# An fp32 metaformer block: the first stage written out as a pipeline over image pairs, and raw x turned to token order through the centring matrix

## What is computed

```python
def reference(x, ...):                       # x: (32, 64, 56, 56) fp32
    x = x + conv_ref(_ln_c(x), weight, gamma, beta, bn_mean, bn_var)
    t = _to_tokens(x)                        # (32, 3136, 64)
    t = t + ffn_ref(_ln_t(t), sigma, phi, M_u, M_phi_plus, M_phi_minus, log_weights, gumbel)
    return _from_tokens(t, x)

def conv_ref(x, ...):                        # its residual is the normalized x
    out = sign(x)
    out = conv3x3(out, scale * sign(weight)) # padding 1
    return out * inv[c] + (beta - mean * inv)[c] + x

def ffn_ref(x, ...):                         # a spectral unit: FFT convolution of length 4096 over
    ...                                      # the tokens with 16 filters, a 64x64 matrix for each
```

## Time and profile before

| | us |
|---|---|
| median of three runs | 1637.34 (1632.1 to 1641.38) |
| the profiled execution | 1645.81, its span 1643.9 |
| prepare | 0 to 61.8 |
| first stage | 61.8 to 760.1 |
| mixing stage: preparing M, then the units | 760.1 to 796.5, then to about 1340 |
| busy over the span | PE 80%, DVE 67%, ACT 50%, POOL 40% |

### The profile page before, as it was taken

How to read it: one execution, slowest core, us unless ns; L and a number is a source line. 1 busy time by engine, 2 the same in 40 slices (tenths; PEclk the granted TensorE clock), 3 DMA queues, 4 the chain that set the end, 5 groups by cost and what they waited for, 6 DMA issues and landing times. The chain is left out here.

```text
span 1643.9 us, 36604 instructions
## 1 busy us (share of the span) xinstructions
PE 1320.2 (80%) x13633; PEld 902.3 (55%) x13633; DVE 1098.6 (67%) x1492; ACT 815.8 (50%) x1517; POOL 659.5 (40%) x665
## 2 busy tenths in 40 slices
PE   1467888888888888867897999999999991867756
PEld 1244444444444444432686898998998980433323
DVE  5268888888888888886665777775776760433323
ACT  0344666666666666644554565564565650222222
POOL 1046777777777777760012232322323222000000
PEclk9988999999999999985798999999999996878888
DMA  9911334434444334335189998997989876987883
GB/s 144 70 70 65 129 128 129 129 131 130 129 129 132 129 132 129 108 100 154 56 231 270 279 288 261 272 261 218 276 252 269 264 217 215 362 345 273 345 338 159
DMA packets 187818, 317.15 MB, mean 193 GB/s; under 512 B 23029, under 2 KB 162647, under 8 KB 171159
## 3 DMA queue, kind: packets, MB, share of 16 engines
q1 hardware_dynamic: 173190, 257.40, 52.9%
q0 software_dynamic: 14592, 59.26, 10.0%
HBM read 162.86 MB, written 153.76 MB: 193 GB/s over the span
## 5 line engine op out<-in xcount | busy, mean ns | idle before, releaser
L939 POOL DMA_DIRECT2D w_scratch<-wf x256 | 151.3, 595 | 467.2 <-ACT y_sb L1117 406.7
L998 PE MATMUL ring<-v_mov,m_sta 105*128 105x128 f16 x4096 | 234.0, 219 | 0.0
L998 PEld LDWEIGHTS ring<-v_mov,m_sta 105*128 105x128 f16 x4096 | 231.5, 98 | 0.4
L554 PE MATMUL p_conv<-signs_padded,conv_w 128*128 128x448 bf16 x1008 | 198.2, 354 | 11.7 <-ACT conv_y L620 11.7
L658 POOL TENSOR_TENSOR conv_y<-conv_y,x_in 128x448 f32<-128x448 f32 x112 | 180.5, 1626 | 40.1 <-ACT conv_y L620 32.6
L1134 DVE COPY hf<-ring 128x512 f32<-128x512 f32 x256 | 168.7, 689 | 26.8 <-PE ring L998 25.8
L1117 ACT ACTIVATE hf<-ring 128x512 f32<-128x512 f32 x256 | 153.0, 598 | 58.6 <-PE ring L998 56.7
L526 PE MATMUL p_rt<-ident,conv_y 128*98 128x128 f32 x512 | 92.0, 319 | 96.9 <-DVE x_t L739 53.9
L1267 PE MATMUL p_out<-w_in,last_masked 128*98 128x512 f32 x256 | 143.4, 645 | 25.4 <-DMA w_in<-w_scratch 25.4
L1323 ACT ACTIVATE out_sb<-p_turn 128x392 f32<-128x392 f32 x128 | 62.7, 498 | 196.6 <-PE p_turn L1279 188.2
L554 PEld LDWEIGHTS p_conv<-signs_padded,conv_w 128*128 128x128 bf16 x1008 | 96.6, 97 | 115.6 <-issue 18.9
(11 more groups left out here) (140 smaller groups left out, 2228.4 us busy)
## 6 DMA issues: line engine op xcount, KB each, us to landing
z_in<-z_scratch SPq DMA_DIRECT2D x32, 1076.5 KB, 8.4
z_scratch<-z_sb SPq DMA_DIRECT2D x16, 2048.0 KB, 8.9
y_scratch<-y_sb SPq DMA_DIRECT2D x32, 1024.0 KB, 9.2
yt<-y_scratch SPq DMA_DIRECT2D x64, 512.0 KB, 6.5
w_scratch<-wf POOLq DMA_DIRECT2D x256, 128.0 KB, 5.4
w_in<-w_scratch SPq DMA_DIRECT2D x8, 4096.0 KB, 15.0
x_in<-in_x SPq DMA_DIRECT2D x16, 1568.0 KB, 11.0
x_scratch<-x_t SPq DMA_DIRECT2D x16, 1568.0 KB
```

The lines of the kernel that those rows point to most:

```text
L554: mm = nc.tensor.matmul(p_conv[:, c % 2, 0:CW], keep["conv_w"][:, t, :], pad[:, rows, t % 3:t % 3 + WID], start=(t == 0), stop=(t == 8))
L939: nc.gpsimd.dma_start(w_units[u, h, s, c], wf[64 * c:64 * c + 64, 2 * h + s].rearrange("p (g n) -> p g n", n=256)).then_inc(w_stored, 16)
L998: mm = nc.tensor.matmul(bank[:, 2 * NF * i:2 * NF * i + 2 * NF], m_sta[:, 2 * e + 1 - n:2 * e + 3 - n, :].rearrange("k b d -> k (b d)"), v ...
```

## The change

**The loop.** The first stage is written out without loops, in 20 turns (`TURNS`, -2 to 17). Turn `it` convolves pair `it`, turns x of pair `it+1` to token order, centres pair `it+2` for its signs, finishes the second normalization of pair `it-1` and makes step 1 of pair `it-2`.

**Raw x.** `x_cen` and its seven copies a pair are gone. `turn_x` makes, in place of each transpose of centred x, a product of raw x (stationary) with the centring matrix (moving), which centres and turns at once. x of three pairs is held in `x_all`; its rows are overwritten in place by the residual.

**Work on other engines.** ScalarE's seven scalings and GpSimd's seven additions of the residual become one bias on the whole pair on ScalarE (`add_bias`) and seven operations on VectorE (`residual`), which read the convolution from PSUM. Both roots of a turn are made together on 128 columns: a square root on ScalarE, a reciprocal and three small steps on VectorE. The scaling of `xc_t` moves from VectorE (2 x 2048 columns) to GpSimd (4 x 1024), both squarings of u are on ScalarE, step 1 goes through `p_xt`.

**The ends.** In `prepare` the three filter stores are one with rows three times as long, a third x is loaded, and the loads of M go to the end of turn 14. The maxima of M stand on VectorE behind the last pair.

The diff, cut to what is spoken of:

```diff
-        filt_z = sb("filt_z", [NROW, NA, NK])
+        filt_z = sb("filt_z", [NROW, NA, 3, NK])
...
-            for q in range(2):
-                sp.dma_start(keep["x_in"][q][:], x_pairs[q]).then_inc(keep["x_loaded"][q], 16)
-
-            sp.wait_ge(filt_saved, 4)
-            for copy_of in range(3):
-                at = NIMG * CH + NK * copy_of
-                sp.dma_start(d["z"][:, :, at:at + NK], filt_z[:]).then_inc(filt_stored, 16)
-            for row, n, src in ((0, KF, d["M_plus"]), (KF, KF, d["M_minus"]), (2 * KF, KU, d["M_u"])):
-                for i in range(NBR):
-                    rows, m = slice(i * NK + row, i * NK + row + n), src[i].rearrange("k d e -> k (d e)")
-                    if i < NBR - 1:
-                        sp.dma_start(keep["m_raw"][0][rows, :], m).then_inc(keep["m_loaded"], 16)
-                    else:
-                        for h in range(2):
-                            sp.dma_start(keep["m_raw"][1][KI * h + row:KI * h + row + n, :],
-                                         m[:, h * M_COLS // 2:(h + 1) * M_COLS // 2]).then_inc(keep["m_loaded"], 16)
-            sp.wait_ge(filt_stored, 48)
+            for q in range(3):
+                sp.dma_start(keep["x_all"][:, TOK * q:TOK * q + TOK], x_pairs[q]).then_inc(keep["x_loaded"][q], 16)
+
+            sp.wait_ge(filt_saved, 12)
+            sp.dma_start(d["z"][:, :, NIMG * CH:ZCOLS], filt_z[:].rearrange("p a t k -> p a (t k)")
+                         ).then_inc(filt_stored, 16)
+            sp.wait_ge(filt_stored, 16)
...
-                nc.vector.tensor_copy(filt_z[:, 8 * c:8 * c + 8, :].rearrange("p a k -> p (a k)"),
-                                      p_f[:, c, 0:8 * NK]).then_inc(filt_saved, 1)
+                for t in range(3):
+                    nc.vector.tensor_copy(filt_z[:, 8 * c:8 * c + 8, t, :],
+                                          p_f[:, c, 0:8 * NK].rearrange("p (a k) -> p a k", k=NK)
+                                          ).then_inc(filt_saved, 1)
...
+            for it in TURNS:
+                if there(it - 2):
+                    sp.wait_ge(z_saved, NTOK * (it - 2) + NTOK)
+                    sp.dma_start(d["z"][:, :, 128 * (it - 2):128 * (it - 2) + 128],
+                                 z_sb[:].rearrange("p c (a n) -> p (c a) n", n=128)).then_inc(z_stored, 16)
+                if not there(it):
+                    continue
+                if there(it + 3):
+                    sp.wait_ge(rt_ready, NTOK * it + NTOK)
+                    sp.dma_start(x_of(it + 3), x_pairs[it + 3]).then_inc(x_loaded[it % 3], 16)
+                sp.wait_ge(x1_done, NTOK * it + NTOK)
+                sp.dma_start(d["x1"][it], x1_t[:].rearrange("p c n -> p (c n)")).then_inc(x1_stored, 16)
+                if it == NPAIR - 2:
...
+            def turn_x(q, c):
...
+                if c < 2 and there(q - 4):
+                    pe.wait_ge(z_saved, NTOK * (q - 4) + NTOK - 1 + c)
+                elif NTOK * q + c >= 2:
+                    pe.wait_ge(xt_copied, NTOK * q + c - 1)
+                    pe.wait_ge(xt_squared, NTOK * q + c - 1)
+                for j in range(ACH):
+                    a = ACH * c + j
+                    mm = nc.tensor.matmul(p_xt[0:NB, c % 2, 128 * j:128 * j + 128], x_of(q)[:, a:TOK:NA],
+                                          keep["center"][:], start=True, stop=True)
+                mm.then_inc(xt_ready, 1)
...
+            def step1(q, c):
+
+                if c >= 2 or not there(q + 3):
+                    if NTOK * q + c >= 2:
+                        pe.wait_ge(z_saved, NTOK * q + c - 1)
+                else:
+                    pe.wait_ge(xt_copied, NTOK * (q + 3) + NTOK - 1 + c)
+                    pe.wait_ge(xt_squared, NTOK * (q + 3) + NTOK - 1 + c)
+                if c % 2 == 0:
+                    if q == NPAIR - 1 and c >= 4:
+                        pe.wait_ge(u_last, c // 2 - 1)
+                    else:
+                        pe.wait_ge(u_done, 4 * q + c // 2 + 1)
+                nc.tensor.matmul(p_xt[:, c % 2, :], keep["step1"][:, c // 2, :], u_t[q % 2][:, c, :],
+                                 start=True, stop=True).then_inc(z_ready, 1)
+
...
+            for it in TURNS:
+                for c in range(NCONV):
+                    if there(it):
+                        convolve(it, c)
+                    if c < 4 and there(it + 1):
+                        turn_x(it + 1, 2 * c)
+                        turn_x(it + 1, 2 * c + 1)
+                    if c >= 4 and there(it - 2):
+                        for k in range(3 * (c - 4), min(3 * (c - 4) + 3, NTOK)):
+                            step1(it - 2, k)
...
+                    if c < NCONV and there(it + 2):
+                        center(it + 2, c)
+                    if there(it):
+                        turn_r(it, c)
...
+            def square2(q, h):
+
+                if h == 0:
+                    act.wait_ge(u_centered, q + 1)
+                else:
+                    act.wait_ge(u_centered_late, 2 * q + 2)
+                if there(q - 1):
+                    act.wait_ge(ssq2_done, 2 * (q - 1) + h + 1)
+                v = slice(HALF * h, HALF * h + HALF)
+                nc.scalar.activation(sq2[:, v, :], u_t[q % 2][:, v, :], ACT.Square).then_inc(sq2_done, 1)
+
+            def add_bias(q):
+
+                act.wait_ge(cen_ready, NCONV * q + NCONV)
+                act.wait_ge(xt_ready, NTOK * q + NTOK)
+                nc.scalar.activation(x_of(q), x_of(q), ACT.Identity, bias=keep["bn"][:, 1:2]).then_inc(biased, 1)
+
             def save_z(q, c):
...
+            def square_root(it):
+
+                s = roots_of(it)
+                act.wait_ge(var_done, it + 2)
+                nc.scalar.activation(deviation[:, s], var[:, s], ACT.Sqrt).then_inc(deviation_done, 1)
+
+            for it in TURNS:
+                if there(it + 1):
+                    for c in range(NTOK):
+                        copy_x(it + 1, c)
+                if there(it - 1):
+                    for h in range(2):
+                        square2(it - 1, h)
+                if there(it + 1):
+                    add_bias(it + 1)
+                if there(it - 2):
+                    for c in range(NTOK):
+                        save_z(it - 2, c)
...
+                    if there(it + 2):
+                        signs(it + 2, c)
+                    if c == 1 and (there(it + 1) or there(it - 1)):
+                        square_root(it)
...
+                if there(it - 2):
+                    q = it - 2
+                    pool.wait_ge(root_done, it + 1)
+                    for c in range(4 if q < NPAIR - 1 else 2):
+                        scaled_by_root(nc.gpsimd, u_t[q % 2], c, 64).then_inc(u_done, 1)
+                if there(it - 1):
+                    q = it - 1
+                    pool.wait_ge(mean2_done, q + 1)
+                    if there(q - 2):
+                        pool.wait_ge(z_ready, NTOK * (q - 2) + NTOK)
+                    for c in (2, 3):
+                        v = slice(2 * c, 2 * c + 2)
+                        nc.gpsimd.tensor_tensor(u_t[q % 2][:, v, :].rearrange(groups, n=CH),
+                                                x1_t[:, v, :].rearrange(groups, n=CH),
+                                                mean2[:, 16 * c:16 * c + 16].unsqueeze(2).to_broadcast([NB, 16, CH]),
+                                                ALU.subtract).then_inc(u_centered_late, 1)
+                if there(it):
+                    pool.wait_ge(root_done, it + 1)
+                    for c in range(4):
+                        scaled_by_root(nc.gpsimd, xc_t[it % 2], c, 0).then_inc(normed, 1)
             pool.wait_ge(peaks_done, len(M_PIECES))
             nc.gpsimd.partition_all_reduce(keep["peak"][:], keep["peaks"][:], 128, bass.bass_isa.ReduceOp.max)
...
+            def residual(q, c):
+
+                g = NCONV * q + c
+                if c == 0:
+                    dve.wait_ge(biased, q + 1)
+                dve.wait_ge(conv_ready, g + 1)
+                v = x_of(q)[:, CW * c:CW * c + CW]
+                nc.vector.scalar_tensor_tensor(v, p_conv[:, g % 2, 0:CW], keep["bn"][:, 0:1], v,
+                                               ALU.mult, ALU.add).then_inc(r_done, 1)
+
...
+            for it in TURNS:
+                before, now, after = there(it - 1), there(it), there(it + 1)
+                if before:
+                    mean_sum(it - 1, 0)
+                if now:
+                    residual(it, 0)
+                if before:
+                    mean_sum(it - 1, 1)
+                    mean_scale(it - 1)
+                if now:
+                    residual(it, 1)
+                if before:
+                    center_u(it - 1)
+                if now:
+                    residual(it, 2)
+                if after:
+                    sums1(it + 1, 0)
+                if now:
+                    residual(it, 3)
+                if after:
```

(22 more changed lines are left out.)

428 lines of the change are left out of this document (153 added, 275 removed).

## The result

The changed kernel takes 1679.4 us (median of 4 runs, 1674.3 to 1683.5) against 1637.5 for the kernel before: a ratio of 1.026, 95% interval 1.021 to 1.030. It is slower by 42 us where I forecast 14 us faster, outside my range of 1598 to 1644. Its profiled execution took 1674.3 us (span 1672.6), and I read that one.

The account below looks back on a forecast made before the run. Bound: first stage a loop of handoffs, none of its engines full. Prologue -21.8, pairs +2.6, -9.2, +10.4, -2.3, -5.8, drain +12.0: -14.1 us, from 1645.8 to 1632, carried to the median 1623; own range 1611 to 1636, overall 1598 to 1644.

Parts of the forecast that it names:

- The step that failed: TensorE's turn of x: 64 product instructions at 0.12 us each, 7.6 us, priced by the forward transform.
- The second term: TensorE's half clock after its stall before the third step-1 product: 1.3 us a turn, of the 1.5 it costs now.
- Rival 1: Handoff costs less: TensorE's clock stays up, turn 40.5 us, gain 17 us, time 1606; chance 0.25.
- rival 2: GpSimd and VectorE lock each other out around the late centring: turn 43.6 us, time 1647; chance 0.17.
- rival 3: Prologue gains only half, 10 of 21.8 us, and the drain runs at half clock (+4): 1639; chance 0.08.
- The stall: TensorE stands 4.6 us before the third step-1 product, waiting for ScalarE's save behind two squarings and the bias.
- The bias: ScalarE's one bias operation on 3136 columns a pair: 2.75 us, by the line through copy and squaring.
- No lock from the residual additions: VectorE's seven residuals a turn, one operand in PSUM, add no wait with GpSimd: 0.65 us each.
- The late centring: GpSimd's half of centring u, ending 15.0 us into the turn, 2.3 us before the second squaring wants it.
- The start of the stage: First stage starts at 40 us after one filter store and no M loads, 21.8 us earlier; VectorE's end 34.5.
- The drain: End of the first stage after the last x1 store: 43.2 us, 12.0 more, with the maxima of M last.
- M's preparation: Stretch after the first stage's drain, 36.4 us in the kernel before: taken as untouched, no change.

Follow-up runs that it names:

- the filled stall: Changed kernel plus 18 additional bf16 matmuls a turn on TensorE, between the second and third product of step 1: 1648.9 us.
- the last version: Changed kernel with centred copy kept and transposed, ScalarE's queue reordered, and two residual additions moved up in VectorE's queue: 1508.9 us, ratio 0.924 to the kernel before.
- the product alone: Kernel before, with its transposes of centred x replaced by the product of raw x with the centring matrix and ScalarE's seven copies dropped: 1667.4 us, ratio 1.020.
- the centred copy: Changed kernel, but ScalarE copies each centred chunk out of PSUM and 32 transposes of that copy replace the raw product: 1592.3 us, ratio 0.976.
- both repairs: Changed kernel with the centred copy kept and transposed, and ScalarE's bias and saves put ahead of the squarings: 1523.5 us, ratio 0.932.

## Why the prediction was wrong

**The step that failed** is one term of the sum: "the nearest row of the same shape is the forward transform, 15 in 1.94 us, 0.12 each: 64 of them, 7.6". The shape was nearly the same (the same moving side, 128 stationary columns there and 98 here), the walk through memory was not: the forward transform reads its stationary columns side by side, the product of raw x 32 words apart. In the profile of before the only strided stationaries were those of transposes, and they were no slower than others, so I had a reason not to ask; but the rows did not show a strided one in a true product, and a price that they don't show should have been bounded on both sides. The 64 instructions measured 10.64 us, 0.166 each: 3.04 a turn more, 37 of the 50 us in the twelve pairs. With the columns side by side they take 7.0, so the stride alone makes the difference. In pair 0, where the products run twice, it is some 6.3 of the 7.9 (11.25 for the first 64, from 48.00 to 59.25, where I had 8).

**The second term was mis-sized**: the half clock at 1.3 us, taken from the some 3 us at half clock that followed the old stall of 2.73. Behind the one of 4.6 it costs 2.54 (the filled stall shows it), 1.2 a turn more than I took, 15 us in the twelve pairs. I had the mechanism and its place, and gave 1.50 as the most it could cost. The length of the stall alone does not set the cost: the same 4.61 us are followed by 2.1 in one turn and 3.2 in the next, and one of 1.55, in the last version, by 1.67 or by nothing.

No rival had either. Rival 1 was wrong in its condition, since the clock did not stay up; rival 2 had a time of 1647, and by another way; rival 3 was about the prologue, and the prologue's gain came whole.

**What held.** The stall: 4.6 forecast, 4.61 measured, for the reasons given, down to the queue of squarings and bias. The bias at 2.75 (2.91). No lock from the residual additions, 678 ns against 650, so that rival 2 did not come about. No idle time before the turn of r. The late centring, due 15.0 us into the turn, ended at 14.7 (at 381.4 in the turn that begins at 366.7).

**The start of the stage** came out right, 40 forecast and 39.9 measured, and that is partly luck. The store, due at 39, had landed by 38.2. What ended last was VectorE's row in `prepare`, at 39.4, which I had at 34.5 as the lower bound: its stretch up to the filter copies began some 6 us later than in the kernel before, behind a GpSimd operation that now clears two sign tiles (5.73 us in place of 2.90) and itself starts later.

**The drain** came out right, 43.2 forecast and 44.1 measured, and that is luck in part, for I had the maxima of M last. They are not:
```profile
799.03 1.08 ACT L603 ACTIVATE z_sb<-p_xt 128x512 f32<-128x512 f32 x2 [9.04 <-DMA z_scratch<-z_sb]
...
808.50 0.60 ACT L603 ACTIVATE z_sb<-p_xt 128x512 f32<-128x512 f32 x1 [0.36 <-PE p_xt L550]
```
```profile
795.37 4.41 DVE L808 TENSOR_REDUCE peaks<-x_all 105x1 f32<-105x4096 f32 x1
...
804.82 0.22 DVE L812 SCALAR_TENSOR_TENSOR peaks<-peaks,w_row 35x1 f32<-35x1 f32 x1
```
ScalarE cannot save pair 15's z until pair 14's has left the one buffer, 9.04 us of waiting (the products to be saved started at 794.51, so I estimate that some 3 of these are the buffer's own), and its last save starts at 808.50; the maxima are through at 805.0, beside it. They cost nothing there.

**What I left at nothing and was not**: M's preparation is 9.1 us shorter than before. Its code is the same, its clock 0.86 instead of 0.51; its first product takes 1.08 us where the kernel before had 1.55. The kernel before with the product alone had 37.3 us, so it goes with the end of the stage ahead of it, but not simply. Counted alike, from M's first product to the first forward product, it is 27.5 here, 27.4 with the filled stall, 27.5 with the centred copy and with columns 2 apart, 31.9 with columns side by side, 36.4 with the transposes of raw x, and 35.8 to 36.6 in the three versions with ScalarE's queue reordered. In the slow ones of these the first product takes 1.08 as well, and from the second or third on they take 2.0. So some 9 us of the difference in time between two of these versions can lie there and not in the pairs. What decides the clock there stays open.

## What to carry to other kernels

- Price a matmul by a row with the same kind (transpose or product), type, shape *and* stride of the stationary operand. Where no such row exists, take it from both sides; a sum in which 64 instructions a turn hang on one unseen price has no narrow range.
- When a change makes one engine full, what it adds to that engine counts nearly in full: the same product cost 2.6 us a turn where TensorE had waits to spare, and 5.5 in the pipeline. Test the parts of a change apart; here one gained 42 us and the other lost more.
- In an in-order queue, put short operations that another engine waits for ahead of long ones that nobody waits for yet. Reordering two queues, with no operation less, took the pipeline with the centred copy from 1592 to 1509 us.

## What the runs showed of the hardware

- The load of a stationary 128 x 98 in a true fp32 product: 165 ns with columns adjacent, 169 two words apart, 261 to 293 at 4 to 32 words. As a transpose at 32 words: 162.
- An idle stretch of 4.6 us of TensorE in each turn costs 2.5 us more through the clock; 18 matmuls in it buy that back (the clock goes from 0.93 to 1.00). One of 1.55 us is followed by 1.67 us of lost time in five of twelve turns; two of 1.20, in the version with both repairs, leave the clock at 1.00.
- VectorE's residual addition with one operand in PSUM, 128 x 448, takes 678 ns, with GpSimd at work or idle, while its centring with both operands in SBUF takes 3.44 us when it starts behind a GpSimd operation under way; in the earlier trace rows, where it started just ahead of GpSimd's, it took 2.29.
